# Cross-attention and expert block: a new order of TensorE's work within each quarter of an attention step

## The reference, cut to what matters

```python
# x (32,112,256), ctx (32,375,256), 16 heads of 16, 8 experts of 1024
x = x + xattn(v=ctx, k=ctx, q=layernorm(x), mask)      # softmax over 375 keys
x = x + ffn(layernorm(x))                              # rms norm, gate, top-1 of 8 experts
# xattn: q,k,v = in @ w + b; logits = qh.kh / 4 + mask*-1e9; softmax; @ vh; @ wo + bo
# ffn: the expert with the largest gate score: silu(xn @ W1[e] + b1[e]) @ W2[e] + b2[e], times the score
```

## Time and profile before

| | before |
|---|---|
| median of three runs | 1021.65 us |
| the profiled execution | 1021.44 us |
| its span (first to last recorded instruction) | 1019.3 us |
| TensorE matmul busy | 826.0 us, 81% |
| VectorE busy | 614.7 us, 60% |
| GpSimd busy | 522.2 us, 51% |
| ScalarE busy | 434.6 us, 43% |

### The profile page before, as it was taken

One profiled execution on the slowest core, in us unless ns is written; L12 is line 12 of the kernel. 1 busy time (PEld: TensorE's weight loads), 2 busy tenths in 40 slices (PEclk: granted clock), 3 DMA queues, 4 the chain that ended last, 5 costly groups with the idle time before them and its releaser, 6 DMA issues. The chain is left out here.

```text
span 1019.3 us, 31909 instructions
## 1 busy us (share of the span) xinstructions
PE 826.0 (81%) x9355; PEld 620.0 (61%) x9356; DVE 614.7 (60%) x1938; ACT 434.6 (43%) x1089; POOL 522.2 (51%) x766
## 2 busy tenths in 40 slices
PE   1688898898898898889889889940089999999994
PEld 0356666666666666666666666620067777778773
DVE  4467777777777777777777776542044454444442
ACT  0245555555555555555555555510033333333331
POOL 0455577577577567667657657545622223232231
PEclk9779999999999999999999999975589999999998
DMA  8757756756765775775775675436322222222210
GB/s 243 192 133 192 196 143 182 193 156 171 183 178 160 183 189 146 182 203 134 183 208 139 173 200 140 98 143 255 91 61 67 70 58 69 68 65 76 62 50 7
DMA packets 124528, 143.72 MB, mean 141 GB/s; under 512 B 13274, under 2 KB 116550, under 8 KB 123464
## 3 DMA queue, kind: packets, MB, share of 16 engines
q1 hardware_dynamic: 119048, 132.15, 48.6%
q0 software_dynamic: 4896, 11.05, 3.4%
q10 hardware_dynamic: 544, 0.00, 0.0%
HBM read 100.10 MB, written 44.89 MB: 142 GB/s over the span
## 5 line engine op out<-in xcount | busy, mean ns | idle before, releaser
L1301 DVE CUSTOM_DVE_ANT_0 arena_a<-ps,arena_a 112x375 bf16<-112x375 f32 x256 | 140.5, 549 | 95.1 <-PE ps L905 89.7
L696 ACT ACTIVATE arena_a<-ps 119x448 f32<-119x448 f32 (+1 forms) x256 | 125.8, 546 | 111.9 <-PE ps L929 111.9
L1149 PE MATMUL ps<-arena_b,w_parts 128*128 128x128 f16 x1680 | 148.0, 226 | 5.7 <-issue 4.8
L1149 PEld LDWEIGHTS ps<-arena_b,w_parts 128*128 x1680 | 117.9, 97 | 38.2 <-issue 12.7
L1301 DVE CUSTOM_DVE_ANT_0 arena_b<-ps,arena_a 112x375 bf16<-112x375 f32 x256 | 139.9, 546 | 0.1
L925 PE MATMUL ps<-arena_a 128*128 128x448 bf16 x384 | 137.3, 357 | 0.1
L929 PE MATMUL ps<-arena_a 128*128 128x224 f16 x768 | 136.9, 260 | 0.0
L654 POOL DMA_INDIRECT out<-arena_b x35 | 35.6, 1018 | 180.0 <-DVE arena_b L1471 131.3
L819 ACT ACTIVATE arena_b<-ps,b_sb 128x128 f32<-128x128 f32 x280 | 79.3, 372 | 113.4 <-PE ps L1149 113.4
L1489 DVE TENSOR_SCALAR arena_b<-arena_b 128x512 f16<-128x512 f32 x70 | 31.4, 449 | 129.3 <-ACT arena_b L819 90.9
L538 POOL TENSOR_TENSOR arena_b<-arena_b,arena_a 112x256 f32<-112x256 f32 x32 | 20.5, 640 | 161.3 <-DVE arena_b L1325 161.3
(11 more groups left out here) (170 smaller groups left out, 1558.8 us busy)
## 6 DMA issues: line engine op xcount, KB each, us to landing
arena_a<-k_spill SPq DMA_DIRECT2D x128, 192.0 KB, 3.9
arena_b<-in_L_ffn_W SPq DMA_DIRECT2D x64, 256.0 KB, 4.3
arena_a<-q_spill SPq DMA_DIRECT2D x128, 112.0 KB, 4.4
k_spill<-arena_a SPq DMA_DIRECT2D x32, 384.0 KB, 4.7
arena_b<-in_ctx SPq DMA_DIRECT2D x32, 256.0 KB
w_spill<-arena_b SPq DMA_DIRECT2D x32, 256.0 KB, 4.5
arena_a<-w_spill SPq DMA_DIRECT2D x8, 1024.0 KB, 11.8
arena_a<-in_x SPq DMA_DIRECT2D x64, 112.0 KB, 4.7
```

Of the source, the lines that this page charges most:

```text
L696: nc.scalar.activation(probsT[u % PROB_BUFFERS][0:n], scoreT_bank[c][0:n, 0:QUAD * T], ACT.Exp, scale=1.0 / SCALE_SCORES).then_inc(probs_r ...
L1149: mm = pe.matmul(ps[:, 1 + 2 * parity + f // 4, (f % 4) * P:(f % 4 + 1) * P], w1_parts[:, w_part, bass.ds(e, 1), k, f * P:(f + 1) * P].rea ...
L1301: nc.vector.tensor_tensor_reduce(out=masked_scores[r % 2], in0=shared_bank[r][0:T, 0:S], in1=mask_bias, scale=-1.0, scalar=3.4e38, op0=ALU ...
```

## The change

Six parts, all in the attention stage.

1. TensorE's order in a quarter becomes: maximum products, V products, full-array work, transposed scores of the *next* quad. The last of a step are quad 0 of batch s itself, which were at the head of step s+1.
2. `transpose_maxima` writes to the third score bank (`max_bank`), and waits for all exponentials of batch s-1. It keeps its place after `gate`; after it come the transposed scores of quad 0, which wait for the spread maxima.
3. Full-array work moves within the step: the last chunk of values (`project_values(st, 2)`) from quarter 2 to quarter 3, into bank 3; context goes to banks 4 and 5 instead of 3 and 4; keys 0, heads, keys 1 instead of keys 0, keys 1, heads; attention's transposition between the two first chunks of values; gate to bank 6, with the routed rows.
4. `normalize_queries` is done for batch s+2 in quarter 2 of step s instead of batch s+1 in quarter 0; the first one moves into the prologue. On GpSimd the reciprocal deviation comes before the split of W2.
5. The gate's copy moves from VectorE to ScalarE.
6. ScalarE's order follows: exponentials of quad q+1 at the end of quarter q's list of copies.

```diff
-        proj_bank, tail_bank, max_bank = shared_bank[0:2], shared_bank[2], shared_bank[3]
+        proj_bank, ctx_bank = shared_bank[0:2], shared_bank[1:3]
+        tail_bank, route_bank, max_bank = shared_bank[2], shared_bank[3], scoreT_bank[CHUNKS - 1]
...
 # GpSimd step
-                if st.exists(0):
-                    split_w2(st)
                 if st.exists(-2):
                     queries_rstd(st.batch(-2))
+                if st.exists(0):
+                    split_w2(st)
...
 # ScalarE step
                 if st.exists(2):
                     copy_heads(st)
-                if st.exists(1):
-                    exponentials(st, 0)
                 if st.exists(-1):
                     for j in range(DT):
                         keys_high(st.batch(-1), st.parity(-1), j)
...
-                    exponentials(st, 3)
+                    exponentials(st, 1, 3, (0, 1, 2))
+
+                if st.exists(0):
+                    copy_values(st.batch(0), st.parity(0), 1)
                 if st.exists(-2):
                     for j in range(DT):
                         context_high(st.batch(-2), st.parity(-2), j)
+                if st.exists(3):
+                    copy_gate(st)
+                if st.exists(0):
+                    exponentials(st, 0, 0, (0, 1, 2))
...
 # TensorE
             def transpose_maxima(st):
                 pe.wait_ge(max_ready, H * (st.batch(0) + 1))
+                if st.exists(1):
+                    pe.wait_ge(probs_ready, UNITS * (st.batch(1) + 1))
                 pe.transpose(max_bank[:, 0:T], maxima, ident[0:T, 0:T]).then_inc(maxT_ready, 1)
...
             def transpose_context(b, par, half, j):
                 pe.wait_ge(ctx_loaded[par], CTX_LOADED * (half + 1))
                 if j == 0:
 
-                    wait_count(pe, q_low_ready, DT * b)
-                else:
-
                     wait_count(pe, k_low_ready, DT * b)
                     wait_count(pe, values_copied, 2 * (b - 1) if not isinstance(b, int) or b > 1 else 0)
...
 # TensorE step; its new form
+                scores(st, 0)
+                values(st, 2, 3)
+                project_keys(st, 0)
+                transpose_heads(st)
+                project_keys(st, 1)
+                scores_transposed(st, 1, 1, (0, 1, 2))
+
+                scores(st, 1)
+                values(st, 1, 0)
+                transpose_queries(st)
+                project_values(st, 0)
+                transpose_attention(st)
+                project_values(st, 1)
+                scores_transposed(st, 1, 2, (0, 1, 2))
+
+                scores(st, 2)
+                values(st, 1, 1)
+                project_queries(st)
+                project_attention(st)
+                transpose_routed(st)
+                scores_transposed(st, 1, 3, (0, 1, 2))
+
+                scores(st, 3)
+                values(st, 1, 2)
+                project_values(st, 2)
+                for j in range(DT):
+                    bank_free(st, 3, 1 + j)
+                    transpose_context(st.batch(-2), st.parity(-2), st.half(-2), j)
+                gate(st)
+                transpose_maxima(st)
+                scores_transposed(st, 0, 0, (0, 1, 2))
...
 # VectorE step
                     row_maxima(st, 0)
                 if st.exists(-1):
-                    normalize_queries(st)
-                    for j in range(DT):
-                        keys_low(st.batch(-1), st.parity(-1), j)
+                    keys_low(st.batch(-1), st.parity(-1), 0)
                 if st.exists(2):
                     divide_heads(st)
+                if st.exists(-1):
+                    keys_low(st.batch(-1), st.parity(-1), 1)
...
                     row_maxima(st, 2)
+                if st.exists(-2):
+                    normalize_queries(st.batch(-2), st.parity(-2))
                 if st.exists(-1):
                     queries_low(st.batch(-1))
...
                         context_low(st.batch(-2), st.parity(-2), j)
-                if st.exists(3):
-                    copy_gate(st)
                 if st.exists(0):
                     spread_maxima(st)
```

More of the change, by code:

```diff
@@ L577, in step @@
                     scale_routed(st)
+                if st.exists(-2):
+                    queries_rstd(st.batch(-2))
                 if st.exists(0):
                     split_w2(st)
-                if st.exists(-2):
-                    queries_rstd(st.batch(-2))
                 if st.exists(1):
@@ L687, in _, with exponentials @@
                                  ).then_inc(setup_copied, 1)
-            def exponentials(st, quad):
-                b = st.batch(1)
+            def exponentials(st, lag, quad, chunks):
+                b = st.batch(lag)
                 wait_count(act, pv_done, QUADS * b + quad - 1)
-                for c in range(CHUNKS):
+                for c in chunks:
                     n, u = ROWS[c], CHUNKS * quad + c
@@ L756, in copy_routed, with copy_gate @@
                 wait_count(act, gate_ready, b)
-                nc.scalar.activation(xrT, max_bank[:, 0:DT * T].rearrange("p (j t) -> p j t", j=DT),
+                nc.scalar.activation(xrT, route_bank[:, 0:DT * T].rearrange("p (j t) -> p j t", j=DT),
                                      ACT.Copy).then_inc(xrT_copied, 1)
+            def copy_gate(st):
+                b = st.batch(3)
+                act.wait_ge(gate_ready, b + 1)
+                nc.scalar.activation(gate_logits[:, bass.ds(b, 1), :].rearrange("p o e -> p (o e)"),
+                                     route_bank[0:T, 0:EXPERTS], ACT.Copy).then_inc(gate_copied, 1)
             def step(st):
@@ L770, in step @@
                 if st.exists(1):
-                    exponentials(st, 1)
+                    exponentials(st, 1, 1, (0, 1, 2))
                 if st.exists(-1):
                     copy_queries_in(st.batch(-1))
+                if st.exists(2):
+                    copy_attention(st)
                 if st.exists(0):
                     copy_values(st.batch(0), st.parity(0), 0)
-                if st.exists(2):
-                    copy_attention(st)
                 if st.exists(1):
-                    exponentials(st, 2)
+                    exponentials(st, 1, 2, (0, 1, 2))
                 if st.exists(-1):
                     queries_high(st.batch(-1))
-                if st.exists(0):
-                    copy_values(st.batch(0), st.parity(0), 1)
                 if st.exists(3):
@@ L910, in transpose_maxima, with scores_transposed @@
                 pe.wait_ge(max_ready, H * (st.batch(0) + 1))
+                if st.exists(1):
+                    pe.wait_ge(probs_ready, UNITS * (st.batch(1) + 1))
                 pe.transpose(max_bank[:, 0:T], maxima, ident[0:T, 0:T]).then_inc(maxT_ready, 1)
-            def scores_transposed(st, quad):
-                b, par = st.batch(1), st.parity(1)
-                if quad == 0:
+            def scores_transposed(st, lag, quad, chunks):
+                b, par = st.batch(lag), st.parity(lag)
+                if quad == 0 and 0 in chunks:
                     pe.wait_ge(max_rows_ready, b + 1)
-                    pe.wait_ge(q_stacked[par], Q_MOVED * (st.half(1) + 1))
-                    pe.wait_ge(k_stacked[par], K_MOVED * (st.half(1) + 1))
-                for c in range(CHUNKS):
+                    pe.wait_ge(q_stacked[par], Q_MOVED * (st.half(lag) + 1))
+                    pe.wait_ge(k_stacked[par], K_MOVED * (st.half(lag) + 1))
+                for c in chunks:
                     u = CHUNKS * quad + c
@@ L1098, in step @@
                 if st.exists(1):
-                    values(st, 1, 2)
+                    scores_transposed(st, 1, 3, (0, 1, 2))
                 if st.exists(0):
@@ L1312, in spread_maxima, with normalize_queries @@
                                         ).then_inc(max_rows_ready, 1)
-            def normalize_queries(st):
-                b, par = st.batch(-1), st.parity(-1)
+            def normalize_queries(b, par):
                 wait_count(dve, xnT_ready, b)
```

55 lines of the change are left out of this document (17 added, 38 removed).

## The result

The changed kernel takes 1088.8 us in the median of four runs (1088.13 to 1093.32), against 1021.2 us for the kernel before on the same chip: a ratio of 1.067, 95% interval 1.065 to 1.069. It is slower, by more than the forecast's 1072 and within its range. The profiled execution has a span of 1087.6 us, 68.3 more than before.

The account below looks back on a forecast made before the run. TensorE was nearest to the bound, with 2 us of waits a step. At +1.56 a step, 29 steps give +45, edges +5; +50 on the old time makes 1072 us, range 1040 to 1105.

Parts of the forecast that it names:

- the chain named: Quarter 3: second value copy, context, ScalarE's copy, context halves, spread, then transposed scores; 6.83 against 4.57 us, +2.26.
- the walk: The whole step laid out quarter by quarter from old trace times: 21.00 us against 19.44.
- Quarter 0: First quarter of a step: ends on the second key block's VectorE copy, 5.36 us against 5.70, -0.34.
- that the order is a mistake: Quarter 0: putting keys 1 behind the heads spoils it, leaving TensorE 0.6 us idle.
- Quarters 1 and 2: Middle quarters: 4.40 us against 4.30 (+0.10), and 4.41 against 4.95 (-0.54), mostly from the moved chunk of values.
- The sum: All four quarters of a step: 21.00 us against the mean of 19.44, +1.56 a step.
- rival 4: TensorE clock: idle stretches of 1.6 us bring the low level in part of each step; +55, 1127 us; chance 0.05.
- rival 1: Quarter 2: normalisation slips behind GpSimd's split of W2; +0.9 us a step, +26, 1098 us; chance 0.18.
- the free case: Quarter 2: normalisation runs unhindered by GpSimd's split of W2, about 0.4 us, with 0.3 us of room.
- Rival 2: Quarter 3: the wait for the second value copy does not bind; -0.82 us a step, -24, 1048 us; chance 0.08.
- Rival 3: Whole step: quarter 3's chain shrinks under other work, quarters run at TensorE's pace; -42, 980 us; chance 0.07.
- The edges: Steps 0, 30, 31 and the normalisation in step -1: +5 us together, bounds 0 and +9.

Follow-up runs that it names:

- f1: Changed kernel, context waiting only for the first value copy, maxima transposed between context transpositions and spread before VectorE's context halves: 1019.2 us, ratio 0.996.
- g1: Changed kernel with the maxima spread ahead of the context halves, the wait for the second value copy left in: 1026.5 us, ratio 1.005.
- e3: Changed kernel with keys 0 and 1 together ahead of the heads, as before the change: 1090.8 us, ratio 1.065.
- e4: Changed kernel with five unread matmuls of 512 columns behind the transposed maxima, in TensorE's idle stretch: 1065.4 us, ratio 1.041.
- e2: Changed kernel with quad 0's transposed scores back behind the next step's maximum products: 1071.0 us, ratio 1.046.
- f2: Changed kernel with context waiting only for the first value copy and five unread matmuls in the idle stretch: 1045.0 us, ratio 1.020.
- e1: Changed kernel, but the first context transposition waits only for the first value copy of its batch: 1058.7 us, ratio 1.035.
- f3: Changed kernel with two unread matmuls behind the transposed maxima, in TensorE's idle stretch: 1071.8 us, ratio 1.047.

## Why the prediction was right, and where its size was off

**The direction and its place.** Right: the loss is quarter 3, by the chain named. The forecast had 6.83 us for it, undisturbed quarters measure 6.57 and 6.76, and its links came where the walk put them: context 2.65 (2.59), end of the chain 5.68 (5.52), first start of the next step 6.83 (6.76). f1 and g1 show that the order of context and spread is what makes it dear.

**Quarter 0.** Forecast 5.36, measured 5.12 and 5.20. The second key block was priced too high: ScalarE's copy began 1.16 after the block's start (322.17 less 321.01), not 1.24, and the heads took 0.45, not 0.53. The last hand-over was priced too high as well: TensorE starts 5.12 into the quarter, 0.13 after VectorE's second `keys_low` (4.38, for 0.61), not the 0.24 taken from the division. That the second `keys_low` comes last was right, though TensorE waits 0.24 for it and not 0.6 (6.1 us over 25 steps in the table above); that the order is a mistake was not (e3).

**Quarters 1 and 2.** 4.40 and 4.41 forecast, 4.41 and 4.51 measured. In quarter 2 the transposed scores took 1.24 to the start of maximum products instead of the 1.15 that they took up to a context transposition; so it did in quarters 1 and 3 too, where other items came out shorter than in the walk.

**The sum.** 21.00 forecast, 20.75 measured at full clock, against 19.44. Had the clock held, the kernel would take about e4's 1065.4, 7 us under the forecast.

**What was mis-sized: the clock.** The forecast took it at nothing and gave rival 4 a chance of 0.05 at +55 us. It happened, at less than half that price: 23.4 us by e4, in eight steps of the steady stage above all. The reason given against it, that the clock had stayed at 1.00 with waits of 1 us, was no reason for 1.6 us; e2 shows that it would not have been one for 1.01 us either, where a second wait stands close by. With the clock and the walk's error the sum closes: 1072 + 23 - 7 = 1088. That the range held the result is in part luck: it left rival 4 out, and its room above 1072 was there for rival 1, which did not happen in the steady stage.

**The rest.** The normalisation ran beside W2's split as in the free case. The row of its line in the changed kernel, over all 32 of its executions (shortest, median and longest in ns):

```profile
L1320 DVE TENSOR_SCALAR arena_a<-arena_a,arena_b x32: 406/407/1235, 29.8 to 676.8; 112x256 f32<-112x256 f32 x32
```

And one meeting with GpSimd, from the changed kernel's timeline:

```profile
309.57 0.41 DVE L1320 TENSOR_SCALAR arena_a<-arena_a,arena_b 112x256 f32<-112x256 f32 x1
309.75 1.25 POOL L532 TENSOR_TENSOR arena_b<-arena_b 128x512 f16<-128x512 f32 x1
```

It took 0.41 us, the median of all; it was GpSimd's L532 that grew, from the 1.16 of its counterpart to 1.25. Only in steps 0, 1 and 2, whose quarters have other lengths, did it meet GpSimd's work at another point, and took 1.24, 0.90 and 0.69. So rival 1 did not happen from step 3 on, by 0.2 us of room (its start lay 0.18 and 0.24 ahead of L532 in turn). Rival 2 (the wait does not bind) is refuted by f2, 20.4 us against a forecast price of 24. Rival 3 (faster) decided once quarter 3 gains less than 0.8 us: in f1 it gains 0.6 (5.10 and 5.30 against 4.57 and 4.63), and the kernel is faster, though by 0.4% and not by 4%; quarters 0 to 2 run as they do in the changed kernel. The edges were +5 in the forecast and +9.8 in the trace: 7.9 in steps 0 and 1, less 1.1 for the earlier start, and 3.0 behind step 31's start. Step 0 is 3.9 longer at a clock that is no lower than before (0.66 against 0.58), step 1 is 4.0 longer at 0.80 against 0.90.

**Open.** Why every other step's quarter 3 is longer, by 0.06 us before and 0.2 after (loop bodies of two steps; 0.3 in e1), was not tried. Nor was why the slow steps come in groups with undisturbed ones between; they are evenly spaced (steps 9 and 10, 15 and 16, 21 and 22, then 25 and 29; in e2 steps 10, 16, 22 and 28; in f3 steps 10, 18 and 26). Open is also whether one wait counts or several together. In the orders in which the clock fell, TensorE's two waits of quarter 3 (for the value copy and for VectorE at its end) are together 2.2 us (the changed kernel), 1.8 (f3), 1.6 (e1) and 1.6 (e2) in the steps concerned; where it did not fall they are at most 1.3 (e4), 1.0 (g1) and 1.0 (the kernel before). In e1, e2 and f3 each fall up to 640 us comes in the step of a pair whose wait for VectorE is the longer one (1.59 against 1.26, 1.01 against 0.83, 1.21 or more against 1.01). e1 comes nearest to changing the sum alone (2.2 to 1.6, with the longest wait at 1.64 and 1.59), and loses 13.7 us by the clock instead of 23.4. And it was not tried whether the order of kinds of matmuls has a part in it; e4 shows only that it does not lower the clock by itself.

## What to carry to other kernels

Where an engine's order is rewritten, lay out each period as a walk with one time per hand-over, and look first for the item whose release starts the next period: work that ran beside it and is moved behind it is paid in full. Check what a shared count really waits for when one of its members moves; here one count too many cost 20 us. An order that gives TensorE more idle time in one place than the old kernel had can have a second price, the clock, which the old trace cannot show; in e2 that happened though no single wait was longer than the old kernel's.

## What was not expected of the hardware

Idle stretches of 1.4 to 1.6 us once in a step of 20.7 us brought stretches at the low clock in some steps, and so did 1.2 us (f3), and 0.56 and 1.01 us close together (e2); 1.01 us in a step of 19.4 did not. Eight steps of 22.7 to 23.5 us instead of 20.75 were most of the price, and five matmuls of 512 columns whose results nobody reads bought 23.4 us back. The Trainium skill (TensorE: Matmul & The Clock Gate, section "HAM oscillation") describes a return of the low clock, again and again, for waits on transfers that are longer than TensorE's work between them. The trace agrees that waits bring it back, but here they are for VectorE, at most 1.7 us long, and inside a stream that has matmuls for 85% of the time.
